# A mixture-of-experts layer: the 64-row third of each down product as two column halves in the two partition halves of a PSUM bank

## The reference, cut to what matters

```python
probs = softmax(xr @ Wg); gate_vals, expert_idx = top_k(probs, 2)
# place of each token in its expert's 320 rows; what is beyond 320 is dropped
dispatched = xr[...].reshape(8, 320, 256)
h = relu(einsum('ecd,edf->ecf', dispatched, w1))       # 256 -> 1024
expert_out = einsum('ecf,efd->ecd', h, w2)             # 1024 -> 256
out = sum over the two choices of gate_val * expert_out[row of the token]
x = x + tanh(g) * out
```

## Time and profile before

| | us |
|---|---|
| median of 3 runs | 944.16 |
| lowest, highest | 941.50, 945.82 |
| profiled execution: span from first to last instruction | 941.6 |
| TensorE busy in it | 735.4 |
| DVE, ACT, POOL busy | 551.5, 372.5, 343.9 |

### The profile page before, as it was taken

One profiled execution on the slowest core, in us unless ns is written; L12 is line 12 of the kernel. 1 busy time (PEld: TensorE's weight loads), 2 busy tenths in 40 slices (PEclk: granted clock), 3 DMA queues, 4 the chain that ended last, 5 costly groups with the idle time before them and its releaser, 6 DMA issues.

```text
span 941.6 us, 14328 instructions
## 1 busy us (share of the span) xinstructions
PE 735.4 (78%) x5159; PEld 509.5 (54%) x5204; DVE 551.5 (59%) x1280; ACT 372.5 (40%) x673; POOL 343.9 (37%) x364
## 2 busy tenths in 40 slices
PE   5987899992567777777797992693876489999998
PEld 3444554561535555555665881362444457777776
DVE  2897847329779999989368453928676520000004
ACT  4002033222389898989520333241663122111220
POOL 2931310654137776767303715500230170000124
PEclk9997899996779898988699996696988579999999
DMA  6311217895029999999811668100013144333413
GB/s 223 127 56 46 49 42 226 195 125 48 1 44 181 170 179 163 179 164 179 174 45 45 152 122 279 42 2 0 1 42 139 46 118 142 104 103 104 149 45 117
DMA packets 139218, 102.78 MB, mean 109 GB/s; under 512 B 109714, under 2 KB 124300, under 8 KB 137102
## 3 DMA queue, kind: packets, MB, share of 16 engines
q1 hardware_dynamic: 130472, 79.10, 34.8%
q0 software_dynamic: 7760, 22.16, 11.7%
q10 hardware_dynamic: 918, 0.62, 0.2%
HBM read 65.34 MB, written 11.33 MB: 81 GB/s over the span
## 4 chain that ended last, share of the span: by engine, by line
PE 33%; issue 13%; DVE 11%; ACT 4%; DMA 3%; POOL 3%; POOLq 0%; DVEq 0%; ACTq 0%
PE psum L2291 8%; PE psum L2273 7%; PE psum L1608 3%; DVE xnT L1399 2%; PE psum L214 2%; PE psum L1885 2%; ACT both L1292 2%; DMA both<-grouped_y_dram,idx 1%; POOL both L561 1%; PE psum L1623 1%; PE psum L1208 1%; PE psum L1468 1%; DMA both<-both 1%; PE psum L614 1%; PE psum L628 1%
## 5 line engine op out<-in xcount | busy, mean ns | idle before, releaser
L1399 DVE TENSOR_SCALAR_CACHE_REDUCE xnT<-psum,both 128x1024 bf16<-128x1024 f32 x128 | 157.7, 1280 | 16.4 <-PE psum L1208 16.2
L1119 POOL TENSOR_SCALAR both<-both 128x1024 f16<-128x1024 f32 x128 | 133.7, 1045 | 83.7 <-ACT both L1292 76.8
L1292 ACT ACTIVATE both<-psum,both 128x1024 f32<-128x1024 f32 x128 | 153.7, 1208 | 14.8 <-DVE xnT L1399 14.4
L1208 PE MATMUL psum<-both 128*128 128x512 bf16 x215 | 77.5, 432 | 40.2 <-ACT both L1292 32.9
L2358 DVE COPY both<-psum 128x256 f32<-128x256 f32 (+1 forms) x21 | 8.9, 422 | 141.5 <-PE psum L2291 141.5
L2291 PE MATMUL psum<-both 128*128 128x256 f32 (+1 forms) x384 | 85.5, 380 | 0.6 <-issue 0.6
L1229 PEld LDWEIGHTS psum<-both 128*128 128x128 f16 x1024 | 64.1, 99 | 26.5 <-issue 12.7
L2273 PE MATMUL psum<-both 128*128 128x320 f32 x256 | 74.4, 445 | 3.8 <-ACT both L549 3.8
L2291 PEld LDWEIGHTS psum<-both 128*128 128x128 f32 (+1 forms) x384 | 65.4, 172 | 19.8 <-issue 3.7
L2327 ACT ACTIVATE both<-psum 128x320 f32<-128x320 f32 x64 | 28.0, 437 | 121.3 <-PE psum L2273 121.3
L1229 PE MATMUL psum<-both 128*128 128x16 f16 x1024 | 68.4, 172 | 9.2 <-DVE xn L1408 6.9
(11 more groups left out here) (373 smaller groups left out, 1525.2 us busy)
## 6 DMA issues: line engine op xcount, KB each, us to landing
both<-in_l_experts SPq DMA_DIRECT2D x50, 384.0 KB, 4.0
both<-in_l_experts SPq DMA_DIRECT2D x16, 1024.0 KB, 5.7
grouped_y_dram<-both SPq DMA_DIRECT2D x31, 128.0 KB
ctok<-in_ctx SPq DMA_DIRECT2D x2, 1024.0 KB, 8.1
both<-kpad_dram SPq DMA_DIRECT2D x1, 2048.0 KB, 8.0
moe_xn_dram<-xn POOLq DMA_DIRECT2D x4, 512.0 KB, 3.9
moe_y_dram<-both POOLq DMA_DIRECT2D x7, 256.0 KB, 4.9
both<-both SPq DMA_TRANSPOSE x96, 3.5
```

Source lines behind the costliest of these rows:

```text
L1119: nc.gpsimd.tensor_scalar(r2[n % RSLOTS2], e2[:, n % ESLOTS2, :], 255.0, HALF_BASE, ALU.mult, ALU.add).then_inc(sem("r2_ready"), 1)
L1208: last = nc.tensor.matmul(bank[2 * (n % SRING2) + half], qz2[:, h % 2, h // 2, t * P:(t + 1) * P], kT2[:, h // 2, half * 512:(half + 1) * ...
L1292: nc.scalar.activation(e2[:, n % ESLOTS2, :], scores_at(n), ACT.Exp, bias=bias2[:, n:n + 1], scale=s2[:, t * H2 + h:t * H2 + h + 1], accum ...
L1399: nc.vector.tensor_scalar(scaled2[n % 2], scores_at(n), ns2[:, t * H2 + h:t * H2 + h + 1], None, ALU.mult, ALU.min, accum_out=bias2[:, n:n ...
```

## The change

For experts 0 to 6 the third of 64 rows is computed in two halves of 128 columns. The first half's output is at partitions 0 to 63 of the bank and the second half's at partitions 64 to 127, both in columns 0 to 127. DVE copies the 128 x 128 block in one operation, and POOL stores it with two DMAs of 64 rows x 128 columns. The last expert keeps the old form and gets a third buffer in `y7`, which ScalarE no longer has to wait for; the diagonal moves into the space of `xnT`.

```diff
-        y7 = r.f32(2, 3, D)
+        y7 = r.f32(3, 3, D)
-        moe7.diag = r.f32(NT, P)
+        moe7.diag = xnT[:, 0, :].rearrange("p (t n) -> p t n", t=NT)
+        Y7_STORES = 16 * (1 + DC)
...
                 for f in range(FC7):
-                    last = nc.tensor.matmul(bank[4 + j][0:n, 0:D], h7[:, i, f, lo:lo + n],
-                                            w7[:, i, DC * FF7 + f * D:DC * FF7 + (f + 1) * D], start=(f == 0), stop=(f == FC7 - 1))
+                    w = w7[:, i, DC * FF7 + f * D:DC * FF7 + (f + 1) * D]
+                    if j == 2 and e < LAST7:
+                        for side in range(DC):
+                            last = nc.tensor.matmul(bank[4 + j][side * n:(side + 1) * n, 0:P], h7[:, i, f, lo:lo + n],
+                                                    w[:, side * P:(side + 1) * P], start=(f == 0), stop=(f == FC7 - 1))
+                    else:
+                        last = nc.tensor.matmul(bank[4 + j][0:n, 0:D], h7[:, i, f, lo:lo + n], w, start=(f == 0), stop=(f == FC7 - 1))
                 last.then_inc(sem("down7_done"), 1)
...
-            act.wait_ge(sem("y7_stored1"), 32 * (E7 // 2 - 1))
...
-            nc.vector.memset(y7[P // 2:P, :, 2, :], 0.0).then_inc(sem("own_ready"), 1)
+            nc.vector.memset(y7[P // 2:P, 2, 2, :], 0.0).then_inc(sem("own_ready"), 1)
...
-                        dve.wait_ge(sem(f"y7_stored{i}"), 32 * (e // 2))
-                    nc.vector.tensor_copy(y7[0:n, i, j, :], bank[4 + j][0:n, 0:D]).then_inc(sem("y7_ready"), 1)
+                        dve.wait_ge(sem(f"y7_stored{i}"), Y7_STORES * (e // 2))
+                    if j < 2:
+                        nc.vector.tensor_copy(y7[:, i, j, :], bank[4 + j][:, 0:D]).then_inc(sem("y7_ready"), 1)
+                    else:
+                        nc.vector.tensor_copy(y7[:, i, j, 0:P], bank[4 + j][:, 0:P]).then_inc(sem("y7_ready"), 1)
...
-                pool.dma_start(moe7.y_dram[e * C7 + 2 * P:(e + 1) * C7, :], y7[0:C7 - 2 * P, i, 2, :])\
-                    .then_inc(sem(f"y7_stored{i}"), 16)
+                for side in range(DC):
+                    pool.dma_start(moe7.y_dram[e * C7 + 2 * P:(e + 1) * C7, side * P:(side + 1) * P],
+                                   y7[side * P // 2:(side + 1) * P // 2, i, 2, 0:P]).then_inc(sem(f"y7_stored{i}"), 16)
```

More of the change, by code:

```diff
@@ L2298, in own_rows @@
                     last = nc.tensor.matmul(bank[t // 2][:, t % 2 * D:(t % 2 + 1) * D], own7[:, j, t * P:(t + 1) * P],
-                                            y7[:, LAST7 % 2, j, :], start=(j == 0 and t % 2 == 0), stop=(j == 2), skip_group_check=True)
+                                            y7[:, 2, j, :], start=(j == 0 and t % 2 == 0), stop=(j == 2), skip_group_check=True)
                     if j == 2 and t % 2:
@@ L2329, in l3f_scalar @@
                         moe7.turn_rows_scalar(act, e + 1, TURN7_AFTER.index(f), bank[7])
-            act.wait_ge(sem("y7_stored1"), 32 * (E7 // 2 - 1))
             for j, (lo, n) in enumerate(JT7):
                 act.wait_ge(sem("down7_done"), 3 * LAST7 + j + 1)
-                nc.scalar.copy(y7[0:n, LAST7 % 2, j, :], bank[4 + j][0:n, 0:D]).then_inc(sem("own_y"), 1)
+                nc.scalar.copy(y7[0:n, 2, j, :], bank[4 + j][0:n, 0:D]).then_inc(sem("own_y"), 1)
         def l3f_vector(dve, seq):
@@ L2379, in l3f_gpsimd2 @@
                     .then_inc(sem(f"y7_stored{i}"), 16)
-                pool.dma_start(moe7.y_dram[e * C7 + 2 * P:(e + 1) * C7, :], y7[0:C7 - 2 * P, i, 2, :])\
-                    .then_inc(sem(f"y7_stored{i}"), 16)
-            pool.wait_ge(sem("y7_stored0"), 32 * (E7 // 2))
-            pool.wait_ge(sem("y7_stored1"), 32 * (E7 // 2 - 1))
+                for side in range(DC):
+                    pool.dma_start(moe7.y_dram[e * C7 + 2 * P:(e + 1) * C7, side * P:(side + 1) * P],
+                                   y7[side * P // 2:(side + 1) * P // 2, i, 2, 0:P]).then_inc(sem(f"y7_stored{i}"), 16)
+            pool.wait_ge(sem("y7_stored0"), Y7_STORES * (E7 // 2))
+            pool.wait_ge(sem("y7_stored1"), Y7_STORES * (E7 // 2 - 1))
             moe7.gather_gpsimd(pool)
```

## The result

The changed kernel takes 931.76 us (median of 4 runs, 926.74 to 932.96) against 943.85 before: a ratio of 0.9865, with a 95% interval of 0.9835 to 0.9894. The profiled execution took 932.96 us with a span of 931.1.

A forecast was written before the change was run, and what follows sets the result against it. TensorE was taken to bound the kernel until expert 6 is done. -10.6 us of matmuls and +0.4 for the store tail make -10.2: span 941.6 to 931.4, plus 2.6 carried over gives 934.0 us, range 931 to 947.

The forecast's parts named there:

- this case's own range: Total time if the halves overlap: 932 (12.0 us saved, no tail) to 937.5 (7.8 saved, tail of 1.1).
- TensorE bounds the stage, so what is taken off it is taken off the end: Down products of experts 0 to 6, 777.00 to 909.20 us: TensorE busy 129.90 of 132.20, so its savings shorten the total.
- The halves overlap: Third of 64 rows, experts 0 to 6: matmuls of the two column halves run beside each other; chance 0.42.
- 17 slots of 0.114 us, 1.94 per third, 10.6 us in all: Order A1 A2 B1 B2 per chunk (halves A, B; instructions 1, 2): A2 pairs with B1, saving 1.51 us per expert.
- the row with full-width loads: Nearest profile row, fp32 matmuls with 128 columns: 3.8 us for 32, so starts every 0.114 us.
- Loads under the slots "with nothing to spare": Halved third on TensorE: two 64-column weight loads, 0.11 us, fit under one matmul slot of 0.114 us.
- +0.4 us for the third issue behind expert 6: POOL's extra store issue delays the gathers by 0.56 us, less 0.13 for DVE's shorter copy; bounds 0 to +1.1.
- Nothing for the stores of experts 0 to 5, the diagonal, the zeroing, ScalarE's wait and the weights: Smaller changes on POOL, DVE, ScalarE and DMA: hidden by waiting or free capacity, so nil.
- strict order: Rival: B1's load begins only after A2 has begun; 5.7 us saved, less 0.4: 938.9 us (936.5 to 941); chance 0.22.
- no overlap: Rival: the halves take turns at 0.108 to 0.114 us; 944.6 to 946.0 us, say 945.3; chance 0.21.
- emptying at each change of half: Rival: each of 15 changes within seven thirds costs 0.15 us, 15.7 us in all: 960.3 us; chance 0.10.
- no load hides: Rival: all 32 loads of a third are exposed, +1.77 us per expert, +12.4 in seven: 957.0 us; chance 0.05.

The follow-up runs named there:

- the first experiment: Changed kernel with both column halves written to partitions 0 to 63, columns 0 to 127 and 128 to 255 of the bank: 944.98 us, ratio 1.000 to the kernel before.
- the runs of 2, 4 and 8 chunks: Changed kernel with that many of the eight chunks (two matmuls each) issued on one half before the other: 932.11, 940.02 and 942.44 us, one run each.

## Why the prediction was right, and where it was off

The time, the sign and the mechanism held: 934.0 was forecast, 931.76 measured, a saving of 12.1 us (943.85 - 931.76) for 10.2. The time lies 0.24 us under this case's own range, 932 to 937.5: the two errors of size below (too little saved, too long a tail) both made the forecast too slow and did not cancel. The overlap itself was a choice with a chance of 0.42, argued from rows that did not show it, so that it came is in part luck. Step by step:

- *TensorE bounds the stage, so what is taken off it is taken off the end*: right. The stage lost 11.9 us for 11.8 us less of matmuls, and what follows kept its 32.4 us.
- *The halves overlap*: right, shown by the kernel with both halves in the same partitions. The 128\*64 pairs start 0.006 us apart and follow each other every 0.109 us.
- *17 slots of 0.114 us, 1.94 per third, 10.6 us in all*: mis-sized. The slots are 0.109 us, and there are 16 of them, since B1 starts with A1 and not with A2: it passes the waiting A2. From the first start to the last it is 1.695 us, where it was 3.288; with the changes of form, 1.90 for 3.59. The saving is 1.69 per expert instead of 1.51. Half of the old form's own pace, 0.108, the other end that the forecast named, was the better neighbour than the row with full-width loads.
- *Loads under the slots "with nothing to spare"*: too narrow. The two halves' loads run at once, four in 0.20 us, so under a slot of 0.109 us stand two loads that run beside each other; in one half loads follow each other every 0.055 us, half a slot.
- *+0.4 us for the third issue behind expert 6*: mis-sized; +0.03 (3.89 to 3.92 us). The path is right, as two more issues showed (+0.82). But the copy got 0.13 shorter, and the last landing 0.39: 32 KB landed in 1.78 us where 64 KB took 2.17. That was the lower bound of the term.
- *Nothing for the stores of experts 0 to 5, the diagonal, the zeroing, ScalarE's wait and the weights*: right as a sum (ratio 1.000 in the first experiment); not tried one by one.

Of the rivals, all four fall with the pairs every 0.109 us: *strict order* (B1 overtakes A2), *no overlap*, *emptying at each change of half* and *no load hides*. The program's order does bind, but only where the runs get long: then up to 1.4 of the 1.7 us per expert is lost.

The Trainium skill's rule that I weighed (TensorE: Matmul & The Clock Gate, "What overlaps and what doesn't": weight loads overlap running matmuls only where the row groups differ) is contradicted once more: here loads run under matmuls on the same 128 rows, a third's 32 loads busy for 1.73 us beside its matmuls' 1.97 in the timeline above. The same section calls matmuls strictly ordered in start and end; the runs of 2, 4 and 8 chunks show starts out of the program's order across the halves, by up to three matmuls. Its figure of 2.38 for three column tiles, by which the forecast had estimated 2.17 us for the third, is 0.79 of full pace for each tile; this case's is 0.97, since 3.288 to 1.695 us from first start to last is 1.94 for two.

## What to carry to other kernels

A matmul with 64 output rows cost here as much as one with 128. Cut into two column halves, which are written to the two partition halves of a PSUM bank, the same work took little more than half of the time (1.90 for 3.59 us); tried was only fp32, with 64 rows, and with 40 in layer 0. Issue the halves by turns: runs of up to four matmuls on one half (two fp32 products) cost 0.05 us of the 1.69, runs of 8 cost 0.60 and runs of 16 cost 1.36. Look first at whether TensorE sets the pace where it is done: in layer 3 all of it reached the end, in layer 0 about 1.3 us by the trace and nothing that the medians can tell.

## What the runs showed that was not expected

- A matmul for the free half starts past up to three that wait for the busy one: the third took 1.90, 1.95, 2.50 and 3.26 us for runs of 1, 2, 4 and 8 products on one half, and 3.64 with no second position.
- Weight loads for the two halves run at once: four 64-column fp32 loads within 0.20 us, where in one half two took 0.19.
- One DMA of 64 KB that gathers two partition halves into 64 DRAM rows landed 3.67 us after its issue began, a plain one of 64 KB after 2.17, and two of 32 KB after 2.31, counted from the first's issue.
